# A routed feed-forward layer: whole rows scattered into sorted order, against a sorted list of token numbers, gathered rows and additions in memory

## The reference, cut to what matters

```python
# x: 8192 tokens x 256, after the attention and its residual
xt = layernorm(x)
scores = softmax(xt @ gate_w.T)                      # 8 experts
idx = top_k(scores + gate_b, 2)[1]                   # two experts for each token
weights = take_along_axis(scores, idx)
h1, h3 = xt @ w1[e].T + b1[e], xt @ w3[e].T + b3[e]  # 512 hidden features each
y[e] = swiglu(h1 * h3) @ w2[e].T + b2[e]             # back to 256 features
routed = sum over the token's two experts e of weights * y[e]
shared = the same computation with one more set of weights (sw1, sb1, ...), for every token
out = x + layernorm(routed + shared)
```

## Time and profile before

| What | Value |
|---|---|
| Median of 3 runs | 2693.76 us (2692.63 to 2699.15) |
| Time of the profiled execution | 2669.15 us |
| Its span, first to last instruction | 2667.4 us |
| PE busy over the span | 2195.3 us (82%) |
| ACT, DVE, POOL busy | 1714.7, 1430.9 and 437.1 us |
| TensorE clock, mean granted share | 0.913 |
| Moved by DMA | 401.57 MB, mean 151 GB/s |

### The profile page before, as it was taken

How to read it: one execution, slowest core, us unless ns; L and a number is a source line. 1 busy time by engine, 2 the same in 40 slices (tenths; PEclk the granted TensorE clock), 3 DMA queues, 4 the chain that set the end, 5 groups by cost and what they waited for, 6 DMA issues and landing times. The chain is left out here.

```text
span 2667.4 us, 40193 instructions
## 1 busy us (share of the span) xinstructions
PE 2195.3 (82%) x14379; PEld 1345.5 (50%) x14379; DVE 1430.9 (54%) x2493; ACT 1714.7 (64%) x2084; POOL 437.1 (16%) x553
## 2 busy tenths in 40 slices
PE   3399579999999999999986754999999999999000
PEld 3277423333333333333325533888888888887000
DVE  1166322222222222222216866888888888888587
ACT  1166379999999999999974642555555555554000
POOL 0011100000000000000002324774000000000675
PEclk6699889999999999999998976999999999999555
DMA  8578655555555445555404634776444444452676
GB/s 249 197 272 295 216 91 85 85 85 85 85 85 85 85 85 85 89 89 88 94 19 150 221 125 166 253 250 208 176 168 169 175 168 175 162 179 91 194 247 197
DMA packets 232237, 401.57 MB, mean 151 GB/s; under 512 B 29344, under 2 KB 166056, under 8 KB 221608
## 3 DMA queue, kind: packets, MB, share of 16 engines
q1 hardware_dynamic: 185616, 314.51, 43.9%
q0 software_dynamic: 15632, 43.01, 5.3%
q10 hardware_dynamic: 30864, 42.38, 4.5%
HBM read 243.02 MB, written 156.67 MB: 150 GB/s over the span
## 5 line engine op out<-in xcount | busy, mean ns | idle before, releaser
L1043 ACT ACTIVATE att_prob<-att_scores 128x1024 f32<-128x1024 f32 (+2 forms) x1152 | 1022.6, 1046 | 60.8 <-PE att_scores L995 53.7
L1014 PE MATMUL att_out<-att_prob,att_va 128*32 128x512 f32 (+3 forms) x5120 | 591.7, 543 | 14.7 <-DVE att_prob L1075 14.7
L995 PE MATMUL att_scores<-att_qs,att_ks 50*128 50x512 f32 (+3 forms) x2560 | 469.7, 433 | 40.6 <-DMA att_qs<-guard 38.9
L995 PEld LDWEIGHTS att_scores<-att_qs,att_ks 50*128 50x128 f32 x2560 | 213.1, 185 | 523.3 <-ACT att_prob L1043 429.1
L1075 DVE SCALAR_TENSOR_TENSOR att_prob<-att_prob,att_tri 128x512 f32<-128x512 f32 x224 | 144.7, 687 | 614.3 <-ACT att_prob L1043 614.2
L1624 PE MATMUL moe_ps<-moe_xt_hi,moe_w_hi 128*128 128x512 f32 x896 | 354.9, 396 | 0.0
L1624 PE MATMUL moe_ps<-moe_xt_lo,moe_w_hi 128*128 128x512 f32 x896 | 349.8, 390 | 0.0
L1624 PE MATMUL moe_ps<-moe_xt_hi,moe_w_lo 128*128 128x512 f32 x896 | 349.5, 390 | 0.0
L1819 POOL DMA_INDIRECT comb_yy<-rows_out,keep_slot x128 | 130.8, 1022 | 676.8 <-PEq L1810 636.2
L1690 ACT ACTIVATE moe_h<-moe_ps,moe_wb 128x512 f32<-128x512 f32 x224 | 151.5, 677 | 94.0 <-PE moe_ps L1624 87.7
L944 POOL DMA_DIRECT2D ctx_scr<-att_cout x64 | 48.2, 754 | 996.6 <-DVE att_cout L1093 956.2
(11 more groups left out here) (203 smaller groups left out, 3087.6 us busy)
## 6 DMA issues: line engine op xcount, KB each, us to landing
moe_wraw<-w_scr SPq DMA_DIRECT2D x56, 1412.0 KB, 6.1
qk_parts<-proj_qk SPq DMA_DIRECT2D x64, 512.0 KB, 4.0
moe_xin<-rows_in SPq DMA_DIRECT2D x56, 512.0 KB, 6.9
rows_out<-moe_y ACTq DMA_DIRECT2D x56, 512.0 KB, 2.9
att_qs<-qk_parts SPq DMA_DIRECT2D x180, 128.0 KB
att_ks<-qk_parts SPq DMA_DIRECT2D x180, 128.0 KB
rows_in<-att_zeros SPq DMA_DIRECT2D x16, 1280.0 KB, 20.8
w_scr<-prep_eout ACTq DMA_DIRECT2D x9, 1412.0 KB, 5.1
```

What stands on the lines that cost most here:

```text
L995: last = nc.tensor.matmul(pss[e % SBUFS][:, h, at:at + CH - q0], ks[s][rows, half, kt * P:(kt + 1) * P], qs[s][rows, half, c * CH + q0:(c ...
L1014: last = nc.tensor.matmul(pso[k % 2][strip, q0:], va[team % 2][:, kt, strip], prob[u % PBUFS][:, h, at:at + CH - q0], start=(kt == 0), sto ...
L1043: nc.scalar.activation(prob[u % PBUFS][:, half * 2:half * 2 + 2, start:], pss[e % SBUFS][:, :, start:], ACT.Exp, scale=HD ** -0.5)\
```

## The change

- `route` packs the token's number and its weight side by side (`routed`, two words of 4 bytes), keeps the places in a layout for a list of 128 x `RT` (156) entries, and has five small DVE instructions more and one less. `ROUTED` is 39 instead of 40 (`NEC` = 55).
- `experts`, POOL: 128 indirect DMAs now scatter these 8-byte entries to `sorted_tokens`, which is then loaded as `order`. For each of the 39 routed chunks POOL gathers its rows (4 indirect DMAs of 128 rows from `tokens` into `moe_xin`), three chunks ahead, and adds the weighted result to the shared one in DRAM (4 indirect DMAs with addition, into `sums`). Its order is gather of chunk c + 3, then addition of chunk c. An addition first waits for those of the two chunks before.
- `experts`, ACT: instead of issuing the store of a routed chunk it multiplies the result by the weight, in four instructions of 128 x 256. SP no longer loads routed rows. The loops are written out (`in_turn`).
- `combine`: no gathers, no weights. SP loads the sum and the residual into four buffers each, DVE forms statistics and inverse root, ACT normalises (scale and bias by token), DVE adds the residual, and POOL issues the stores.
- `attend` stored 16 blocks of zeros (1280 KB each) to the routed part of `rows_in`; it now stores two spare chunks of zeros and an empty list.

```diff
-ROUTED = 2 * T // CH + E
+ROUTED = 2 * T // CH + E - 1
+RT = ROUTED * TPC
...
 # route
-                then(V.tensor_reduce(weight[:], tmp[:], AX_X, ALU.add))
+                then(V.tensor_reduce(routed[:].bitcast(F32)[:, :, :, 1], tmp[:], AX_X, ALU.add))
...
-                then(V.tensor_scalar(base[:], base[:], float(NCH * CH), None, ALU.add))
...
+                then(V.tensor_copy(slot[:], slotf[:]))
+                then(V.tensor_scalar(tile[:], slot[:], P.bit_length() - 1, None, ALU.logical_shift_right))
+                then(V.tensor_copy(tilef[:], tile[:]))
+                then(V.scalar_tensor_tensor(slotf[:], tilef[:], -float(P), slotf[:], ALU.mult, ALU.add))
+                then(V.scalar_tensor_tensor(slotf[:], slotf[:], float(RT), tilef[:], ALU.mult, ALU.add))
                 then(V.tensor_copy(slot[:], slotf[:]))
...
 # experts, POOL
-                for c in range(NCH):
+                for t in range(NT):
+                    for r in range(2):
+                        pool.indirect_dma_start(
+                            out=sorted_tokens, out_offset=bass.IndirectOffsetOnAxis(slot[:, r, t:t + 1], 0),
+                            in_=routed[:, r, t, :], in_offset=None).then_inc(listed, 16)
+                pool.wait_ge(listed, 2 * NT * 16)
+                pool.dma_start(order[:].rearrange("p t i -> p (t i)"),
+                               sorted_tokens.rearrange("(p t) i -> p (t i)", p=P)).then_inc(order_loaded, 16)
+                pool.wait_ge(order_loaded, 16)
+
+                def gather(c):
                     n, s = divmod(c, 2)
...
+                    pool.wait_ge(turned[s], n)
+                    for j in range(TPC):
+                        t = (c - NCH) * TPC + j
+                        pool.indirect_dma_start(
+                            out=xin[s][:, j, :], out_offset=None, in_=tokens,
+                            in_offset=bass.IndirectOffsetOnAxis(order[:, t, 0:1], 0)).then_inc(gathered[s], 16)
+
+                def add(c):
+                    n, s = divmod(c, 2)
+                    pool.wait_ge(y_weighed[s], (n - NCH // 2 + 1) * TPC)
+                    for m, d in (divmod(c - 1, 2), divmod(c - 2, 2)):
+                        wait_kept(pool, m + 1, d)
+                    for j in range(TPC):
+                        t = (c - NCH) * TPC + j
+                        pool.indirect_dma_start(
+                            out=sums, out_offset=bass.IndirectOffsetOnAxis(order[:, t, 0:1], 0),
+                            in_=y[s][:, j, :], in_offset=None, compute_op=ALU.add).then_inc(added[s], 16)
+
+                AHEAD = 3
+                for c in range(NCH, NCH + AHEAD):
+                    gather(c)
+                for c in range(NCH, NEC):
+                    if c + AHEAD < NEC:
+                        gather(c + AHEAD)
+                    add(c)
...
 # experts, ACT, store(n, s)
-                    act.dma_start(rout_ch[chunk_of(n, s)].rearrange("a p j d -> p (a j) d"), y[s][:])\
-                        .then_inc(y_stored[s], 16)
+                    c = 2 * n + s
+                    if c < NCH:
+                        act.dma_start(sum_ch[c], y[s][:]).then_inc(y_stored[s], 16)
+                        return
+                    act.wait_ge(order_loaded, 16)
+                    for j in range(TPC):
+                        t = (c - NCH) * TPC + j
+                        nc.scalar.activation(y[s][:, j], y[s][:, j], ACT.Copy,
+                                             scale=order[:].bitcast(F32)[:, t, 1:2]).then_inc(y_weighed[s], 1)
...
 # combine
-                            pool.indirect_dma_start(
-                                out=yy[s][:, r, j, :], out_offset=None, in_=rows_out,
-                                in_offset=bass.IndirectOffsetOnAxis(slot[:, r, t:t + 1], 0))\
-                                .then_inc(gathered[s], 16)
...
+                    pool.wait_ge(done, c + 1)
+                    pool.dma_start(out_ch[c], res[c % OUT][:]).then_inc(stored[c % OUT], 16)
...
+                        nc.scalar.activation(nrm[c % OUT][:, j], acc[c % IN][:, j], ACT.Identity,
+                                             bias=shift[c % 2][:, j:j + 1], scale=rstd[c % 2][:, j:j + 1])\
+                            .then_inc(normed, 1)
...
+                measure(0)
+                for c in range(NCH):
+                    invert(c)
+                    if c + 1 < NCH:
+                        measure(c + 1)
+                    if c:
+                        finish(c - 1)
+                finish(NCH - 1)
```

More of the change, by code:

```diff
@@ L129, in in_rounds, with in_turn @@
         round_(it)
+def in_turn(count, step):
+    for c in range(count):
+        step(*divmod(c, 2), divmod(c + 1, 2) if c + 1 < count else None, divmod(c - 1, 2) if c else None)
 def chunk_of(n, s):
@@ L171, in build @@
         logits = keep.sb("logits", [E, T])
-        weight = keep.sb("weight", [P, 2, NT])
+        routed = keep.sb("routed", [P, 2, NT, 2], I32)
         slot = keep.sb("slot", [P, 2, NT], I32)
@@ L178, in build @@
         project(nc, ident, power, minus_one, heads_of, norms, wqkv, x_ch, qk_parts, v_scr)
[L179 to L183, removed]
+        attend(nc, ident, norms, qk_parts, v_scr, guard, ctx_ch, tokens, sums, sorted_tokens)
+        attention_out(nc, ident, power, minus_one, wo, gw, b_o, x_ch, ctx_ch, x1_scr, tok_ch, logits)
+        route(nc, ident, gate_b, logits, routed, slot, expert_of)
+        experts(nc, ident, tok_ch, tokens, sum_ch, sums, sorted_tokens, w_scr, routed, slot, expert_of)
+        combine(nc, sum_ch, x1_scr, out_ch)
 def prepare_weights(nc, ident, power, minus_one, heads_of, wqkv, wo, gw, w_q, w_k, w_v, w_o, gate_w,
@@ L965, in _ @@
                     load_guard(team)
[L966 to L970, removed]
+                sp.wait_ge(z_made, 3)
+                for spare in (tokens, sums):
+                    sp.dma_start(spare[T:, :].rearrange("(p r) d -> p (r d)", p=P), zeros[:]).then_inc(z_stored, 16)
+                sp.dma_start(sorted_tokens.rearrange("(p t) i -> p (t i)", p=P),
+                             nobody[:].rearrange("p c j i -> p (c j i)")).then_inc(z_stored, 16)
+                sp.wait_ge(z_stored, 16 * 3)
             def loads_by(team):
@@ L1373, in _, with route @@
                 in_steps(dve, NCH, step)
-def route(nc, ident, gate_b, logits, weight, slot, expert_of):
+def route(nc, ident, gate_b, logits, routed, slot, expert_of):
     with ExitStack() as ctx:
@@ L1522, with experts @@
 BOTH_STEP = 12
-def experts(nc, ident, rin_ch, rows_in, rout_ch, w_scr, slot, expert_of):
+def experts(nc, ident, tok_ch, tokens, sum_ch, sums, sorted_tokens, w_scr, routed, slot, expert_of):
     with ExitStack() as ctx:
@@ L1540, in experts @@
         wb = ph.sb2("wb", [P, 2 * FB + D])
+        order = ph.sb("order", [P, RT, 2], I32)
         psT = ph.ps("psT", [P, KT, CH])
@@ L1592, in _ @@
-                for s in range(2):
-                    sp.wait_ge(scattered[s], NCH // 2 * each)
-                with sp.Fori(NCH // 2, NEC // 2) as it:
-                    for s in range(2):
-                        load(it, s, NCH // 2 * each)
             @block.tensor
@@ L1779, in step, with combine @@
                         result(n, s)
-                in_pairs(dve, NEC, step)
-def combine(nc, rout_ch, rows_out, x1_scr, weight, slot, out_ch):
+                in_turn(NEC, step)
+def combine(nc, sum_ch, x1_scr, out_ch):
     with ExitStack() as ctx:
         ph = Phase(nc, ctx, "comb")
-        sh = ph.sb2("shared", [P, TPC, D])
-        x1 = ph.sb2("x1", [P, TPC, D])
-        yy = ph.sb2("yy", [P, 2, TPC, D])
-        acc = ph.sb2("acc", [P, TPC, D])
-        res = ph.sb2("res", [P, TPC, D])
-        wgt = ph.sb2("wgt", [P, 2, TPC])
+        IN, OUT = 4, 2
+        acc = [ph.sb(f"acc{i}", [P, TPC, D]) for i in range(IN)]
+        x1 = [ph.sb(f"x1_{i}", [P, TPC, D]) for i in range(IN)]
+        nrm = [ph.sb(f"nrm{i}", [P, TPC, D]) for i in range(OUT)]
+        res = [ph.sb(f"res{i}", [P, TPC, D]) for i in range(OUT)]
@@ L1804, in combine @@
[L1804 to L1810 removed]
+        shift = ph.sb2("shift", [P, TPC])
+        STEPS = 4
+        loaded = [ph.sem(f"loaded{i}") for i in range(IN)]
```

228 lines of the change are left out of this document (116 added, 112 removed).

## The result

| | Kernel before | Changed kernel |
|---|---|---|
| Median | 2694.84 us (2692.63 to 2699.15, 4 runs) | 2788.25 us (2786.34 to 2792.38, 4 runs) |
| Ratio, 95% interval | | 1.0347 (1.0328 to 1.0366) |
| Profiled execution, its span | 2669.15, 2667.4 us | 2786.34, 2784.3 us |
| Mean granted clock | 0.913 | 0.899 |

The forecast was 2644 us with a range to 2725: the time lies outside of it, on the other side of no change.

The account below looks back on a forecast made before the run. PE's queue was taken to bound `experts` and POOL's queue `combine`. Terms +1.1 - 1.0 - 14.7 + 52.5 + 6.0 - 94.0 = -50.1 us, set against the median 2693.8, gave 2643.7 us, range 2585 to 2725.

Parts of the forecast that it names:

- The list: Start of `experts`, POOL: 128 scatters until 1827, rows ready about 1845, wanted at 1861; hidden with 16 us to spare.
- The stalls: Routed chunks of `experts`: gathered rows come 3.0 us late for PE; 35 steps at 1.5 us more, +52.5 us.
- (W + L) / 2: Routed chunks of `experts`: mean step time from step work and path, (14.7 + 17.7) / 2 = 16.2 us.
- L: Routed chunks: path from a step's opening through additions and gathers until rows are there, 17.7 us; bounds 14.1 to 25.7.
- rival with dear additions: Routed chunks: additions cost more than scatters, at twice the issue and 1 us landing L = 22.5, 2728 us; chance 0.18.
- W: Routed chunks of `experts`: the work of one step, 14.7 us, with nothing added for a lower clock after waits.
- The 24.6 us between median and profile: Whole kernel: median lies 24.6 us above the profiled execution, so the difference was set against the median: 2643.7 us.
- `combine`: Last stretch: 5.2 us a chunk, 95.5 us in place of 189.5, so -94.0; bounds 4.8 and 7.1 us a chunk.
- the end of `experts`: After the last product: multiplications, three more issues, and a landing as long as the store's; +6.0 us.
- In time: Rival, routed chunks: gathers arrive in time, L under 14.7, no stalls; 2591 us; chance 0.20.
- The full lock of DVE on POOL: Rival, routed chunks: each two-SBUF-input DVE instruction shuts POOL out; L = 21.6, stalls 121 us, 2712 us; chance 0.05.
- Slow `combine`: Rival, last stretch: bound by DMAs at today's rate, 7.1 us a chunk, 29 us more, 2673 us; chance 0.07.

Follow-up runs that it names:

- `after_third`: The changed kernel as it stands, run again on another chip than the first measurement: 2675.23 us, ratio 1.0026 to the kernel before.
- plain scatters: The changed kernel with its 156 additions writing without adding, so each row of `sums` holds its last result alone: 2597.17 us, one execution.

## Why the prediction was wrong

**The list, and with it all shared chunks, was costed at nothing: the step that failed.** The prediction calls the list "hidden", with 16 us to spare against the first routed rows, and judges that by POOL's time alone. For POOL that was right: the 128th scatter is issued at 1797 to 1829 us in all runs, where 1827 was forecast. But step 3, beside it, took 126.6 us in place of 14.7: 111.9 us, for which neither the sum nor a rival had a term. What makes the pause stays open; the runs show that it goes with one chip and ends with the list. No row of before could show it: its scatters into `rows_in` move whole rows of 1 KB, in the same place, with PE at full pace. On the three chips without the pause, the step that failed is the next one.

**The stalls: mechanism right, size off.** PE idle before `turn` for a DMA into `moe_xin`, none before chunk 20, as drawn. But 116 us in place of 52.5, by two terms of (W + L) / 2:

- *L.* From the opening at 2194.63 the first addition starts at +2.2 (forecast 2.6), the last gather is issued 14.2 later (11.5), and the rows are there 2.8 after that (3.6): 19.2 in place of 17.7. An addition was taken at a scatter's 0.96 and costs 1.56 at least. 35 x 1.5 / 2 = 26 us. L stays under the 20.6 of the rival with dear additions, which alone would not have made the kernel slower.
- *W.* The clock was costed at nothing, from a wait of 1.15 us. The waits here are 4.4 us, and the step behind each takes 16.0 to 17.6 us, mean 16.7, in place of 14.7: 35 x 2.0 / 2 = 35 us. A row of a short wait was used for a long one. How the stall is spread matters with it: (W + L) / 2 gives the mean step, but not whether it comes as about 1 us in each step, as with plain scatters, where the clock stayed at 0.99, or as 4.4 us in every second, as here.

52.5 + 26 + 35 = 113.5. With both right the sum would have been -50.1 + 61 = +11 us: near what the changed kernel takes on the other chips, +6.4 at a ratio of 1.0026.

**The 24.6 us between median and profile.** The prediction took them over into its forecast of 2643.7 us. The changed kernel doesn't have them: with the pause taken out, its span is 2672.4 us in the pair and 2674.6 on the late chip, beside 2673.7 in `after_third`. This size was wrong too, by 24.6 us on the other side. The forecast missed by 2788.3 - 2643.7 = 144.6 us, which is 117 + 50 = 167 for the terms, less these 24.6, and 2 us between the median and the profiled execution of the changed kernel.

**`combine` and the end of `experts`: sum right, parts off.** The last product is followed by the first load 19.3 us later, not 5.8 (+13.5, forecast +6.0): the last addition is issued at 2694.15, and the load at 2704.82, 10.7 us on, where a store took 4.8. It is not the adding: with plain scatters it is 12.1 us (2503.64 to 2515.77). The prediction had taken their landing to be as long as the store's. `combine` then takes 79.5 us, 4.18 us a chunk, less than the lower bound of 4.8: the timeline of DVE has 4.18 us between `comb_res` of two chunks,

```profile
2755.34 1.22 DVE L1953 TENSOR_TENSOR comb_res<-comb_nrm,comb_x 128x1024 f32<-128x1024 f32 x1
...
2759.52 1.22 DVE L1953 TENSOR_TENSOR comb_res<-comb_nrm,comb_x 128x1024 f32<-128x1024 f32 x1
```

DVE's durations in the earlier trace rows, added up one behind the other, came to 4.7; in the timeline of after they overlap a little, and the gaps are smaller. The 5.0 us that the prediction worked out for DMA, by scaling today's rate to 316 GB/s at full share, do not hold either: in the middle of `combine`, 512 KB loads and stores move 370.

```profile
2725.00:2760.00 35.00, 0.00 (x0) 0.00 (x0) 32.86 (x135) 17.75 (x42) 6.02 (x8) 0.50 1.03 370
```

DVE (busy for 94%) and DMA are both full there. 15 chunks at 4.18 in place of 5.2 are 15.3 us of the 16 by which `combine` came in under its forecast. Together -96.5 against -88.0.

**The rivals.** In time: no. Dear additions: in part. The price came true (mean 1.98 us, a scatter's twice, and over the 1.7 that the prediction named as a sign of being wrong), but L did not reach its 22.5, and the kernel is slower by another cause; that the result fell on this rival's side of no change is luck. The full lock of DVE on POOL: no; L would be 21.6 with additions at a scatter's price, and is 19.2 with dearer ones. In the timeline above the addition beside the weight split takes 3.21 us, and those beside the rest of DVE's work 1.56 to 2.35. Slow `combine`: no.

## What to carry to other kernels

Where work is put on a queue ahead of prefetches, count not only whether the queue can do it all in time but what stands in front of what: here POOL had room, and four buffers instead of two with a gather issued one chunk earlier turned a kernel at 1.0026 of the old time into one at 0.956, and took the stalls away on the late chip too (1.035 to 0.993, with the pause still there). Price a stall of several us with the clock it costs, from a row of a wait of that length; here a wait of 4.4 us cost 2.0 more. And where a term is "hidden", ask not only whether it ends in time but whom it may disturb, and measure on more than one chip. Take the profile and the times that it is set against from the same chip.

## What the runs showed of the hardware

- An indirect DMA that adds costs POOL 1.56 us to issue, one that only writes 0.96, one that gathers 0.95 to 1.02, each where nothing holds it up (128 rows of 1 KB). Beside a DVE instruction of 2.29 us with two SBUF inputs the first rises to 3.21. A scatter of 128 entries of 8 bytes costs POOL 0.96 as well.
- Behind waits of 4.3 to 4.7 us PE worked at the lower clock for about 3 us in one place and 5 in another; each such wait cost 1.4 to 2.9 us more than itself, 2.0 in the mean.
- On one chip of four, 128 scatters of 8-byte entries in a row went with a pause of PE of over 100 us in both kernels that ran there with it, as in the first trace of the changed kernel; in six executions with that list on the other three chips PE was busy for all of 1680 to 1810. The pause ended with the list in all three traces that have it, and indirect DMAs of rows of 1 KB beside written-out code made none in them. What in that chip or its state makes it is open, and so is whether the list is needed for it and whether larger entries would avoid it: the kernels that would tell never ran there.
